# Two edge sums of a graph kernel: GpSimd opens its gathers once for four instead of once for two

## What is computed

```python
x = x + gnn0(layernorm(x))      # agg[row] += edge_weight * (h[col]); then W, bias, batch norm, relu
x = x + ffn0(layernorm(x))      # top half of the nodes through a 256-1024-256 MLP
x = x + gnn1(layernorm(x))      # aggr[row] += edge_val * feat_in[col]; + (1+eps)*feat_in; two products; norm
x = x + moe(layernorm(x))       # 8 experts, the best two for each node

gathered = A_values[:, None] * h[col]
agg = jax.ops.segment_sum(gathered, row, num_segments=A_shape)
```

## Time and profile before

| | us |
|---|---|
| median of 3 runs | 3528.44 (3527.41 to 3529.43) |
| span of the profiled execution | 3521.7 |
| TensorE matmuls busy | 2647.4 (75%) |
| VectorE busy | 2613.3 (74%) |
| GpSimd busy | 2208.3 (63%) |
| ScalarE busy | 1008.4 (29%) |
| GpSimd's gathers, L1081, 1568 of them | 1492.1 busy, 506.5 idle ahead of them |

### The profile page before, as it was taken

How to read it: one execution, slowest core, us unless ns; L and a number is a source line. 1 busy time by engine, 2 the same in 40 slices (tenths; PEclk the granted TensorE clock), 3 DMA queues, 4 the chain that set the end, 5 groups by cost and what they waited for, 6 DMA issues and landing times. The chain is left out here.

```text
span 3521.7 us, 55765 instructions
## 1 busy us (share of the span) xinstructions
PE 2647.4 (75%) x15311; PEld 2239.6 (64%) x15311; DVE 2613.3 (74%) x6603; ACT 1008.4 (29%) x2073; POOL 2208.3 (63%) x2147
## 2 busy tenths in 40 slices
PE   6888466666666665899967677777776569999998
PEld 4777344454444444789945555555555459999997
DVE  6999566666666666969967777777777778888886
ACT  0011000000000002545511111111111168888886
POOL 0455577777777774345557777777777326666664
PEclk9999687878878787899978888888788779999999
DMA  3011433333333332000133333333333447776775
GB/s 98 10 44 33 120 105 105 105 105 105 105 105 105 105 105 73 1 2 31 37 103 111 113 112 111 113 113 111 113 111 113 133 134 216 213 218 211 219 211 140
DMA packets 164679, 389.01 MB, mean 110 GB/s; under 512 B 46378, under 2 KB 95602, under 8 KB 151019
## 3 DMA queue, kind: packets, MB, share of 16 engines
q0 software_dynamic: 99072, 233.49, 24.4%
q1 hardware_dynamic: 65387, 152.94, 12.8%
HBM read 343.97 MB, written 42.98 MB: 110 GB/s over the span
## 5 line engine op out<-in xcount | busy, mean ns | idle before, releaser
L1081 POOL DMA_INDIRECT g_got<-table,e_source x1568 | 1492.1, 952 | 506.5 <-issue 458.9
L1174 PE MATMUL psum<-g_got,g_route 128*128 x3328 | 1087.2, 485 | 642.0 <-DMA g_got<-table,e_source 253.6
L1174 PEld LDWEIGHTS psum<-g_got,g_route 128*128 128x128 f32 x3328 | 760.9, 239 | 888.4 <-issue 763.5
L1107 DVE TENSOR_TENSOR A<-A,psum 128x256 f32 x1664 | 698.5, 420 | 523.6 <-PE psum L1174 345.1
L1090 DVE TENSOR_SCALAR g_route<-columns,e_local,e_weight 128x128 f32<-128x128 f32 x1664 | 472.5, 363 | 17.7 <-issue 12.9
L368 POOL DMA_INDIRECT records<-rec,place x120 | 148.7, 1239 | 220.6 <-ACT rec L580 122.0
L1582 POOL TENSOR_TENSOR f_ht_lo<-f_ht,f_ht_hi 128x512 fp32r<-128x512 f32 x100 | 133.7, 1341 | 187.8 <-ACT f_ht_hi L1531 182.1
L142 PE MATMUL psum<-e_xt_hi,e_w_hi 128*128 128x256 f32 x832 | 238.0, 286 | 5.5 <-issue 5.3
L142 PE MATMUL psum<-e_w_hi,e_ht_hi 128*128 128x256 f32 x832 | 233.1, 280 | 3.1 <-DVE e_w_lo L1981 3.1
L144 PE MATMUL psum<-e_xt_hi,e_w_lo 128*128 128x256 f32 x832 | 233.8, 281 | 0.0
L143 PE MATMUL psum<-e_xt_lo,e_w_hi 128*128 128x256 f32 x832 | 233.7, 281 | 0.0
(11 more groups left out here) (420 smaller groups left out, 5198.5 us busy)
## 6 DMA issues: line engine op xcount, KB each, us to landing
e_w<-in_m_w SPq DMA_DIRECT2D x104, 1024.0 KB, 5.0
g_got<-table,e_source POOLq DMA_INDIRECT x1568, 2.8
expert_table<-g_normal SPq DMA_DIRECT2D x52, 128.0 KB
table<-xn SPq DMA_DIRECT2D x49, 128.0 KB, 1.7
X<-in_x SPq DMA_DIRECT2D x1, 6144.0 KB
table<-f_ring SPq DMA_DIRECT2D x24, 256.0 KB, 2.1
out<-X SPq DMA_DIRECT2D x1, 6144.0 KB
f_w<-in_f_w SPq DMA_DIRECT2D x2, 1024.0 KB, 7.3
```

The lines of the kernel that those rows point to most:

```text
L1081: pool.indirect_dma_start(got[:, c % RING, :], None, rows, bass.IndirectOffsetOnAxis(ap=source[:, c:c + 1].bitcast(U32), axis=0)).then_inc ...
L1107: dve.tensor_tensor(to, to, sums_of(c), ALU.add).then_inc(added, 1)
L1174: ins = pe.matmul(sums_of(c), route[:, c % (GB + GSEM), :], row(got, at[j % GSEM]), start=True, stop=True)
```

## The change

GpSimd's loop over halves of a group is taken out. The wait on `pairs_summed` and the increment of `dma_open` stand once ahead of four gathers instead of once ahead of two. What is waited for is what the last of the four gathers needs. Both edge sums use this code. The gathers themselves, their order, places and counters stay, and so does everything on the other engines.

```diff
-                        for half in range(2):
-                            first = q * GSEM + half * (GSEM // 2)
-                            last_user = first + GSEM // 2 - 1 - RING + (NT - 1)
-                            done = last_user // 2 + 1 if first >= RING else 0
-                            if q >= 8:
-                                done = max(done, first_slot_after(q - 8) // 2 + 1)
-                            wait(pool, pairs_summed, done)
-                            pool.sem_inc(dma_open, 1)
-                            for c in range(first, first + GSEM // 2):
-                                pool.indirect_dma_start(
+                        first = q * GSEM
+                        last_user = first + GSEM - 1 - RING + (NT - 1)
+                        done = last_user // 2 + 1 if first >= RING else 0
+                        if q >= 8:
+                            done = max(done, first_slot_after(q - 8) // 2 + 1)
+                        wait(pool, pairs_summed, done)
+                        pool.sem_inc(dma_open, 1)
+                        for c in range(first, first + GSEM):
+                            pool.indirect_dma_start(
...
```

More of the change, by code:

```diff
@@ L1071, in _ @@
                             pool.wait_ge(edges.sources_made, 1 + (q > 0))
-                        for half in range(2):
-                            first = q * GSEM + half * (GSEM // 2)
-                            last_user = first + GSEM // 2 - 1 - RING + (NT - 1)
-                            done = last_user // 2 + 1 if first >= RING else 0
-                            if q >= 8:
-                                done = max(done, first_slot_after(q - 8) // 2 + 1)
-                            wait(pool, pairs_summed, done)
-                            pool.sem_inc(dma_open, 1)
-                            for c in range(first, first + GSEM // 2):
-                                pool.indirect_dma_start(
-                                    got[:, c % RING, :], None, rows,
-                                    bass.IndirectOffsetOnAxis(ap=source[:, c:c + 1].bitcast(U32), axis=0)
-                                ).then_inc(gathered[q % 8], 16)
+                        first = q * GSEM
[7 more added lines that the diff above has]
+                            pool.indirect_dma_start(
+                                got[:, c % RING, :], None, rows,
+                                bass.IndirectOffsetOnAxis(ap=source[:, c:c + 1].bitcast(U32), axis=0)
+                            ).then_inc(gathered[q % 8], 16)
                 @block.vector
```

## The result

The changed kernel takes 3536.06 us (median of 15 runs, 3530.69 to 3540.14), the kernel before beside it 3528.09 (15 runs, 3525.35 to 3532.43): 8.0 us more, ratio 1.0020 with a 95% interval of 1.0012 to 1.0027. The forecast was 3534.8 us, with a range of 3528.3 to 3538.5.

A forecast was written before the change was run, and what follows sets the result against it. GpSimd's gathers were taken to set the pace. Openings saved gain 0; stalls of 1.50, 1.63, 1.57 and 1.64 us add 6.34 to 3528.44, giving 3534.8 us, range 3528.3 to 3538.5.

The forecast's parts named there:

- What bounds: In both edge sums GpSimd's gathers set the pace, 1.256 us each; a later-ending gather stream ends the sum equally later.
- What is taken away: 392 fewer openings (wait and increment) over both sums, hidden behind the running gather: 0 gain taken, 3.9 us at one bound.
- What is added: At the ring's first turn the first two gathers wait one pair later: four stalls, together 6.34 us slower.
- The release of 0.83 us: Time from the end of the awaited work to the start of GpSimd's released gather: 0.83 us.
- the loop's sum: Ring's first turn, two groups, 10.0 us available: 3.75 + 3.41 + matmuls + 0.83 gives 9.98 fast, 11.64 slow.
- The open term: Whether each sum's second stalling matmul block stays at the slow clock: 0 or 1.64 us a sum; full value taken.
- the two chains: Even and odd gather groups at the ring's first turn, two places each; at most two 1.6 us stalls a sum.
- the block at 467.91: Sum one's matmuls from 467.91 to 475.03; its third group takes at least 1.99 us, so gather 72 doesn't stall.
- One stall in each sum: Rival: the second block runs at 2.4 GHz, so one stall a sum, 3531.5 us; chance 0.27.
- Nothing moves: Rival: release is quicker than 0.83 us or GpSimd catches up, 3528.4 us; chance 0.09.
- openings that cost: Rival: openings take GpSimd's time, 3.9 us gain, giving 3530.9 us with the stalls or 3524.5 without; chance 0.06.
- Tightness beyond group 17: Rival: gather groups 18 and on stall too, five more places at 1.57 us, 3542.7 us; chance 0.13.

The follow-up runs named there:

- second profile of the changed kernel: The changed kernel run again, unaltered, in a later session: 3530.38 us against 3523.23 for the kernel before, ratio 1.0020.
- TensorE kept busy: Changed kernel plus six unit-matrix products ahead of each of slot groups 44 to 60: 3529.08 us against 3526.70 for the kernel before, ratio 1.0002.

## Why the prediction was right, point by point

- **What bounds.** Confirmed. GpSimd's gathers set the pace, and a stall lengthens its sum by itself: the two sums together are 6.5 us longer for 6.24 us of stalls in the second profile of the changed kernel, 2.4 for 3.65 (with gathers 1.0 shorter in all) with two openings and the late wait, 2.3 for 2.2 with TensorE kept busy, and 50.0 for 49.8 with one opening for eight.
- **What is taken away.** The price of 0 for an opening held: removing 384 or 486 of them, or adding 784, left the time within 0.1% and the idle time at 0.305 us. The 0.01 us that I took as the bound for an opening's cost was generous. The cover isn't one gather's 0.95 us, as I wrote, but the lead, 15.3 us for the most part and never below 0.75. The Trainium skill's 50 to 100 ns for reading a semaphore (Advanced Engine Details and Errata, Network/Comms) isn't contradicted: no run here shows the price of a read by itself, and the 0.08 us of an increment lies beside the gathers that are running. The estimate of 20 us or more from it was wrong for this place, by the run with 784 more.
- **What is added.** The later wait is the loss. The two experiments that give the early wait back, one by splitting four groups and one by two more places, both give all of it back, and the late wait alone with all openings kept gives 1.0017.
- **The release of 0.83 us and the loop's sum.** In the second profile the four stalls have the sizes of the sum to within 0.09 us. The release measures 0.77 us from the pair's increment to the gather's start there (pair 28 at 461.48, gather 60 at 462.25) where I took 0.83 from the matmul's end. With eight gathers behind one opening the same terms gave 20 to 26 us a sum and the trace shows 23.5 by the loop, none of it from gather 136 on.
- **The open term.** Second blocks were slow in both profiles of the changed kernel, as chosen (3.77 and 3.78 us in the first; at granted clocks of 0.50 in the second). That the clock sets the size of the stalls is shown by the kernel that keeps TensorE busy, where most blocks took 1.99 us at 1.00 and 2.2 us of stalls were left, and by the small stalls of the late wait with two openings. Which of the two chains stalls isn't fixed: 56 and 64 in sum one of the first profile, 60 and 68 in the second, and the other way round in sum two. I named the places without saying so. "Two stalls in each sum are the most" doesn't hold as a count either: with two openings and the late wait sum two had three, smaller ones.
- **What was off.** 8.0 us were measured beside 6.34, which lies within the interval (1.0012 to 1.0027 is 4.2 to 9.5 us), so the medians show no error of size. One term was too narrow: in the first profile the fourth stall is 2.70 instead of 1.64. I had charged 3.41 us from the last gather's start to the matmuls; there it took 1874.62 - 1870.22 = 4.40:

```profile
1870.22 0.95 POOL L1080 DMA_INDIRECT g_got<-table,e_source  x1 [0.30 <-issue]
...
1874.62 3.78 PE L1173 MATMUL psum<-g_got,g_route 128*128 x8 [5.58 <-DMA g_got<-table,e_source]
```

  The landing came late by 1.0 us; in the second profile it didn't. The trace of the kernel before has landings from 2.6 to 3.9 us after the issue, median 2.8, so it should have been a range and not a value. This one stall doesn't explain the 8.0: the profiled execution took 3532.95 us, 3.1 less than the median.

  Two readings were wrong without harm. The 6.7 us between the span and the median don't lie outside the span: every run of the changed kernel took 1.8 to 1.9 us more than its span, so the profiled execution of the kernel before took some 3523.5, less than any of the 15 runs, and the rest is scatter. And the third group of the block at 467.91 took 1.73 us, not 1.99 or more: gather 72's release lay 0.3 us later than I reckoned, with 1.9 us of room.
- **The rivals.** One stall in each sum: not seen in either profile of the changed kernel, but sum one had one only (1.6 us) in the profile of the late wait with two openings. Nothing moves, and openings that cost: refuted, by the ratios of 1.0020 and by the run with 784 more openings. Tightness beyond group 17: not with four gathers to an opening; none of the profiles at 3.5 ms has such a stall. I gave it too much. I put 0.75 on a change of less than 0.2% (7.1 us); the measured 8.0 us, ratio 1.0020, stands at that bound, and its interval reaches to both sides.

## What to carry to other kernels

A wait that is already met and an increment cost nothing here, because the queue runs ahead of a busy engine: by 15.3 us mostly, by 0.75 at least. Before merging waits to save them, look whether the idle time between neighbours differs with and without one. Merging waits makes the merged one ask for the latest of what its parts asked for, and the price of that is paid where a ring is tightest, here in the first turn, at 8 of 392 groups. Gathers whose opening has hardly any lead are the ones that will stall. To size it, add the loop once around (last fetch, landing, use, release) and compare with the pace, at both levels of TensorE's clock.

## What was not expected of the hardware

- The same program took 3948 us in one session and 3523 to 3528 in others, with VectorE's adds standing still for some 9 us in each step of 16 slots of the first edge sum. They wait for TensorE's increments of `pairs_summed`, which are recorded in bunches and long after their matmuls (9 to 13 us in the step shown). Why is open. The chip's number is the same, 10, for the sessions at 3948.11 and at 3526.70, so that it is a property of a chip isn't shown.
- In the kernel with one opening for eight gathers, gather 113 of both sums, which has no opening ahead, started after 1.67 us of idle time put down to "issue" (the row at 550.64 above). In the kernel before and the changed kernel it starts after 0.30. The same 1.67 us stand ahead of gathers 201, 289, 377, 465, 553, 641 or 729, each 88 further on, in traces of the first session. My reading is that something on the sequencer's side takes over a microsecond there and is hidden where the lead is large; the trace doesn't name it.
- Two profiled executions of one program differed by 5.2 us in the total time of the same 1568 gathers (1497.3 and 1492.4 us), as much as the effect under study.
